# Second weights' low parts, an early high part and an early gelu table in a gated linear attention and feed-forward kernel

## The reference, cut to what matters

```python
x = x + layernorm(attn(layernorm(x)))      # gated linear attention, 4 heads
x = x + layernorm(ffn(layernorm(x)))       # expert e = sequence // 2
# attn: o = scan(S = exp(g) * S + k v^T ; q S), o * rsqrt(mean(o*o) + eps) * rms_w * silu(x Wg), then @ Wo
# ffn:  h = gelu(x w1[e] + b1[e]);  y = h w2[e] + b2[e]   (w1: 256 x 1024, w2: 1024 x 256)
```

## Time and profile before

| | us |
|---|---|
| median of 3 runs | 1126.93 |
| lowest, highest | 1125.78, 1127.64 |
| profiled execution, its own time | 1126.07 |
| its span in the trace | 1124.3 |

### The profile page before, as it was taken

The page is one execution under the profiler, slowest core; times in us unless marked ns, Lnnn a source line. Parts: engine busy times, 40 slices in busy tenths (PEclk is TensorE's granted clock), DMA queues, the critical chain, the costliest instruction groups (busy, mean ns, idle before and its releaser), DMA issues.

```text
span 1124.3 us, 32613 instructions
## 1 busy us (share of the span) xinstructions
PE 1093.1 (97%) x12754; PEld 921.3 (82%) x12754; DVE 852.5 (76%) x2019; ACT 818.4 (73%) x1781; POOL 592.3 (53%) x907
## 2 busy tenths in 40 slices
PE   8999999999999999999999999999999999999977
PEld 6788878888788888878888788887878888788877
DVE  7778587786777968688686877868678686877764
ACT  6887858767687687867778676786767877677644
POOL 7646445564356643565445635456356463454742
PEclk9999999999999999999999999999999999999999
DMA  5100011000120001200002001010010100120000
GB/s 158 41 20 3 19 59 62 20 8 15 59 62 20 14 9 58 63 20 21 26 33 62 21 20 58 2 62 22 20 58 21 44 20 21 58 62 2 8 15 20
DMA packets 32968, 38.91 MB, mean 35 GB/s; under 512 B 3568, under 2 KB 30256, under 8 KB 32816
## 3 DMA queue, kind: packets, MB, share of 16 engines
q1 hardware_dynamic: 32240, 36.30, 9.9%
q10 hardware_dynamic: 576, 0.52, 0.2%
HBM read 28.43 MB, written 8.39 MB: 33 GB/s over the span
## 4 chain that ended last, share of the span: by engine, by line
PE 80%; ACT 7%; DVE 6%; issue 4%; POOL 2%; DMA 1%; SPq 0%; POOLq 0%; ACTq 0%; DVEq 0%
PE ps_big L284 18%; PE ps_big L286 15%; PE ps_big L285 15%; PE ps_out L536 4%; PE ps_level L345 4%; PE ps_level L284 3%; PE ps_out L539 2%; PE ps_level L286 2%; PE ps_level L285 2%; PE ps_state L520 2%; DVE ogT_lo L842 2%; ACT L1548 2%; PE ps_transpose L380 1%; ACT gates L1548 1%; PE ps_transpose L552 1%
## 5 line engine op out<-in xcount | busy, mean ns | idle before, releaser
L1685 POOL TENSOR_TENSOR k_decayed<-k_decayed,block_totals 128x256 f32<-128x256 f32 x192 | 133.4, 715 | 163.2 <-PE ps_level L345 127.0
L873 DVE TENSOR_TENSOR q_blockdiag<-q_blockdiag,block_totals 128x512 f32<-128x512 f32 x192 | 162.0, 851 | 3.2 <-PE ps_level L323 3.2
L284 PE MATMUL ps_big<-w_ff_hi,h_hi 128*128 128x256 f32 x480 | 140.0, 292 | 0.0
L1691 POOL TENSOR_TENSOR rstd<-mean_var,minus_half 128x1 f32<-128x1 f32 x192 | 110.0, 589 | 56.4 <-DVE mean_var L920 55.7
L285 PE MATMUL ps_big<-w_ff_lo,h_hi 128*128 128x256 f32 x480 | 135.6, 283 | 0.0
L286 PE MATMUL ps_big<-w_ff_hi,h_lo 128*128 128x256 f32 x480 | 135.6, 282 | 0.0
L886 DVE TENSOR_TENSOR h_lo<-ps_transpose,h_hi 128x512 fp32r<-128x512 f32 x120 | 79.4, 681 | 45.8 <-ACT h_hi L1270 45.8
L284 PE MATMUL ps_big<-h_hi,w_ff_hi 128*128 128x512 f32 (+1 forms) x272 | 110.6, 407 | 2.8 <-DVE h_lo L842 0.3
L1715 POOL TENSOR_TENSOR w_ff_lo<-w_raw,w_ff_hi 128x256 fp32r<-128x256 f32 (+1 forms) x96 | 104.5, 1106 | 9.3 <-ACT w_ff_hi L1270 9.3
L284 PE MATMUL ps_big<-w_vg_hi,xT_hi 128*128 128x512 f32 x254 | 107.1, 422 | 0.1
L1278 ACT ACTIVATE ps_transpose<-ps_big,ff_b_cols 128x512 f32<-128x512 f32 x120 | 79.2, 660 | 38.2 <-DVE h_lo L886 30.8
(11 more groups left out here) (212 smaller groups left out, 3237.1 us busy)
## 6 DMA issues: line engine op xcount, KB each, us to landing
w_raw<-L_ffn_w SPq DMA_DIRECT2D x16, 1024.0 KB, 6.0
out<-y SPq DMA_DIRECT2D x64, 128.0 KB, 1.7
x_in<-L_attn_x SPq DMA_DIRECT2D x15, 512.0 KB, 3.9
ff_b_rows<-L_ffn_b SPq DMA_DIRECT2D x8, 128.0 KB, 2.1
x_in<-L_attn_x ACTq DMA_DIRECT2D x4, 128.0 KB, 2.5
w_raw<-L_attn_Wv SPq DMA_DIRECT2D x1, 512.0 KB, 6.5
w_raw<-L_attn_Wg SPq DMA_DIRECT2D x1, 512.0 KB, 7.4
y<-L_attn_Wo SPq DMA_DIRECT2D x1, 512.0 KB, 8.3
```

The lines of the kernel that those rows point to most:

```text
L284: nc.tensor.matmul(out, ah, bh, start=(first and i == 0), stop=False)
L873: nc.vector.tensor_tensor(q, q, t.to_broadcast([P, 2, T // (2 * h), h]), ALU.mult)\
L1685: nc.gpsimd.tensor_tensor(k, k, t.to_broadcast([P, m, h]), ALU.mult)\
L1691: nc.gpsimd.tensor_tensor(rs[:, k, c:c + 1], mv[:, k, c, 1:2], mhalf[:, 0:1], ALU.pow)\
```

## The change

Three edits. On ACT, a gelu of one column into `warm` is issued ahead of `gelu(0)` in every step that has a feed-forward part; nobody waits for its result. Also on ACT, `og_hi(1)` is issued ahead of `squares(2)` instead of behind it. On POOL, the pieces 0, 1 and 2 of W2's low part are made at the end of the even step, behind the factors of the third norm; the pieces 4 and 3 follow level 1 of the odd step, and 5, 6 and 7 follow the levels 2, 3 and 4.

```diff
@@ ACT, level phase
+                    if C and i == 1:
+                        nc.scalar.activation(warm[:, :], ident[:, 0:1], ACT.Gelu_apprx_tanh)
                     if C and i < 5:
                         gelu(2 * i - 2)
                         gelu(2 * i - 1)
@@ ACT, second phase
                 if B:
+                    og_hi(1)
                     squares(2)
-                    og_hi(1)
                 if V:
                     g_evac(0, n)
@@ POOL, level phase
                     if C and j == 1 and i < 5:
-                        weight_lo(1, 2 * i - 2, e)
-                        weight_lo(1, 2 * i - 1, e)
+                        weight_lo(1, i + 3, e)
+                    if C and j == 1 and i == 1:
+                        weight_lo(1, 3, e)
@@ POOL, end of a step
                     for c in range(NCH):
                         rsqrt(2, c, "dv_ln3", s, "po_p3")
+                if split_w1:
+                    for part in range(3):
+                        weight_lo(1, part, next_e)
```

## The result

| | us |
|---|---|
| median of 4 runs, changed kernel | 1135.25 (1134.08 to 1136.18) |
| median of 4 runs, kernel before | 1127.29 (1125.78 to 1128.17) |
| ratio, 95% interval | 1.0079 [1.0066, 1.0092] |
| span in the trace, changed kernel | 1132.9 (before 1124.3) |

A forecast was written before the change was run, and what follows sets the result against it. PE, busy for 97% of the span, was taken as the bound. Terms of -7.5, +10.8 and +5.7 summed to +9.0 us, giving 1135.9 us, with an 8-in-10 range of 1124.4 to 1141.5.

The forecast's parts named there:

- early table: One-column gelu on ACT pulls the table load into an idle hole, so gelu(0) starts 1.28 us earlier: -7.5 us.
- moved pieces: Three POOL pieces at the even step's end hold up DVE, making f1(0) 1.35 us later at 8 passages: +10.8 us.
- swap: og_hi(1) ahead of squares(2) leaves ACT standing 0.38 us, moving PE's gap from wo(1) to qp(0): +5.7 us.
- With gelu(0) earlier, f1(2) starts right behind its level: Level phase on PE: f1(2) no longer waits for gelu(0), 0.18 us in each of 15 steps, 2.7 us gained.
- The gap of 0.18: Between level 2 and f1(2) PE takes 0.87 us, against 0.69 after level 3, in every step with a feed-forward part.
- (b): f1(0) to f2(0) takes 0.60 us longer in odd steps; closing it in all 8 gains 4.8 us.
- DVE stands until the POOL instruction is over, and then needs 0.15 or 0.55: Meetings with POOL pieces: a DVE scaling ends 0.15 us behind the piece, a two-operand instruction 0.55; three cost 1.37.
- (b) is paid once: The thinner POOL list in odd steps, 5 pieces not 8, works on (b) too, but adds no second gain.
- POOL gives way: Rival: DVE wins the meetings with POOL's pieces, which then cost 1.8 us; total 1126.9 us, chance 0.12.
- The 0.38 of ACT: ACT stands 0.38 us before og_hi(1), waiting for ogt(1), with everything up to v_evac(1) queued behind.
- Only to wait for v_evac(1): PE arrives early at qp(0) and waits for v_evac(1), which ends 0.38 us later; wait of some 0.7 expected.

The follow-up runs named there:

- experiment 5: Kernel before plus the early table, with one piece instead of three behind the third norm and seven in the odd step: 1123.13 us, ratio 0.9972.
- experiment 4: Changed kernel without the swap of og_hi(1), so early table and moved pieces together: 1130.03 us, ratio 1.0033 to the kernel before.
- experiment 2: Kernel before with only og_hi(1) moved ahead of squares(2): 1131.05 us, ratio 1.0045.
- experiment 3: Kernel before with only the pieces of W2's low part moved: 1133.35 us, ratio 1.0062.
- experiment 6: Kernel before plus the early table, pieces in their old place, and three write-only POOL fills behind the third norm: 1132.5 us, ratio 1.0057.
- experiment 9: Kernel of experiment 8 with v_evac(1) moved ahead of squares(3) on ACT: 1120.5 us, ratio 0.9952 to the kernel before.
- experiment 11: Kernel of experiment 8 with the copy v_evac(1) on DVE behind og_lo(1) instead of on ACT: 1116.62 us, ratio 0.9915 to the kernel before.
- experiment 8: Kernel before plus the early table, with og_hi(1) between the second and third square of chunk 2: 1118.36 us, ratio 0.9935.
- experiment 10: Changed kernel with v_evac(1) moved ahead of squares(3) on ACT: 1136.9 us, ratio 1.0094 to the kernel before.

## Why the prediction was right

1135.25 were measured and 1135.9 were forecast. The signs of all three parts held, each by an experiment of its own. That the two totals are so near is in part luck, as the last point says. Their sizes, in us over the launch:

```
part                 forecast   measured
early table            -7.5       -6.2
moved pieces          +10.8       +9.8
swap                   +5.7       +4.7
stall and clock, step 4   0       +1.6 in this profile
```

- **The early table.** "With gelu(0) earlier, f1(2) starts right behind its level" holds (0.69). The terms were too large, for two reasons. The gap of 0.18 was there in every step, 0.86 to 0.88 against 0.69, but closing it gave 0.12: some 0.04 comes back in f1(2) itself, 2.97 us long now and 2.93 before, and the rest in the groups behind it. A gap was priced at its full length. The 0.60 of (b) was read from step 5 alone, whose level phase gained 0.73 where most odd ones gained 0.67; over all odd steps 0.55 is what closed. And the forecast had the load itself 1.3 us earlier; it starts 2.21 earlier, at the beginning of the hole, and gelu(0) 1.32.
- **The moved pieces.** "DVE stands until the POOL instruction is over, and then needs 0.15 or 0.55" was measured as 0.15 (experiment 5) and 0.56. The three operations came out 0.40, 0.27 and 0.55 longer, 1.22, and PE lost 1.22. The forecast had 1.37 (and went on with 1.35), since it gave both later pieces 0.64 behind the end of the operation that they had waited for. Measured are 0.59 and 0.60, and from the first one's start to the last one's end (496.57 to 498.92) the three took 2.35, not 2.47. The remark that (b) is paid once is experiment 4. That POOL gives way is out as the rival had it: ln3(3), k update and q_update stood in each profile in which a reading piece met them. POOL stood too, but briefly, 0.05 for the second piece and 0.19 for the third.
- **The swap.** The 0.38 of ACT measured 0.39 from start to start and 0.40 in PE. The idle time in the row is only 0.30, since an instruction's duration contains some 0.1 in which the next one would have begun. "Only to wait for v_evac(1)" named one of two rows: gp(1) comes first, wants the bank that g_evac(0) empties, and takes 0.54 of the wait; qp(0) has the last 0.19, where some 0.7 were forecast. Both hang on the same late list of ACT, so the sum held. What was not seen are the 0.09 us that come back up to wo(3) in each step, 1.3 us in all. That nobody waits for the later o_rstd(2) held as far as PE's list shows it.
- **What came from elsewhere.** The forecast was nearer than its terms. Three terms too large by 1.3, 1.0 and 1.0 leave only 0.7 too much, because the first of them is a gain. Step 4 put 1.6 on top in the profiled execution, of which fill and drain took 1.3 back. None of these was foreseen.

## What to carry to other kernels

When an engine loads a table while it waits for its input, a one-column activation of the next function ahead of the wait pulls the load into the hole, here for 0.65% of the time. An idle stretch of POOL is not free if DVE is on the critical path in it: count the DVE instructions that meet a POOL instruction which reads (here 0.27 to 0.55 us each), and charge each with what is left of the POOL instruction and the tail of DVE's own. Before a copy is moved ahead of other work on a full engine, ask whether its input is there; if the engine stands, every later evacuation that a matmul waits for is late by as much.

## What the runs showed that was not expected

**The clock.** In each profile PE stalls once for 2.1 to 2.5 us, in step 4 within level 1, with nothing released ("issue"). In some the granted clock falls near the end of that stall and in others it does not. Busy time by stretches around it, with the granted clock as the third number from the end; changed kernel, then the one before:

```profile
287.00:290.50 3.50, 3.50 (x88) 2.72 (x90) 3.48 (x11) 2.24 (x5) 0.70 (x2) 1.00 0.89 331
290.80:294.10 3.30, 0.91 (x72) 0.76 (x62) 1.86 (x4) 1.99 (x4) 0.74 (x1) 1.00 0.21 82
294.10:299.40 5.30, 5.30 (x86) 4.06 (x77) 2.18 (x4) 1.84 (x3) 0.85 (x2) 0.68 0.02 5
```

```profile
285.00:289.50 4.50, 4.50 (x98) 3.32 (x101) 4.45 (x14) 2.93 (x6) 1.28 (x3) 1.00 0.84 312
289.50:292.40 2.90, 0.77 (x66) 0.65 (x55) 1.92 (x4) 0.58 (x2) 0.74 (x1) 1.00 0.18 66
292.40:298.00 5.60, 5.39 (x92) 4.27 (x93) 2.22 (x5) 3.42 (x5) 2.05 (x3) 1.00 0.02 4
```

0.68 is a mean over time at the lower level (1.2 GHz) and at the higher (2.4 GHz). It costs f1 of step 4 some 1.6 us in six of the thirteen profiles (the change and experiments 2, 3, 5, 6 and 9). The length of the stall does not decide it: 2.08 and 2.39 us went before a fall (experiment 9 and the change), 2.09, 2.40 and 2.47 before none (experiments 11, 8 and 10). Nor does the version alone: of 17 runs of the kernel before on one chip, the nine whose mean granted clock was 0.998 or more took 1125.4 us on the mean, the eight at 0.997 or less 1127.1. Where in those runs the clock fell is not on record. What decides it, and what the stall itself waits for, is open. A difference of 0.15% between two profiles of this kernel can be this alone.

**Fills that don't let go.** A scaling on DVE that meets three fills in a row stands for 1.93 us, and for 0.81 if it meets three subtractions in a row. Why DVE gets its turn behind the first instruction in one case only is open.
